# Loading x's first pair first and in halves, its norm ahead of the bias masks, and the zeros for the masked values written by ScalarE

## What is computed

```python
x = x + xattn0(layernorm(x), ctx)          # 16 heads of 16; biases bq, bk, bv, bo
x = x + ffn0(layernorm(x))                 # ternary weights, 8-bit activations
x = x + xattn1(layernorm(x), ctx)          # two attentions of 16 heads of 32, each with its own feed-forward
x = x + moe(layernorm(x))                  # 8 experts, each token goes to one
```

```python
xh = (x - mean) / sqrt(var + 1e-5)
q  = xh @ Wq + bq                          # Wq 256 x 256
k  = ctx @ Wk + bk                         # Wk 128 x 256
v  = ctx @ Wv + bv
```

## Time and profile before

| | us |
|---|---|
| median of three runs | 1157.76 |
| the three runs | 1154.86, 1157.76, 1159.51 |
| the profiled execution | 1160.95 |
| its span, first to last instruction | 1159.2 |
| TensorE busy in the span | 1056.4 |
| VectorE, ScalarE, GpSimd busy | 527.4, 459.0, 272.2 |

### The profile page before, as it was taken

How to read it: one execution, slowest core, us unless ns; L and a number is a source line. 1 busy time by engine, 2 the same in 40 slices (tenths; PEclk the granted TensorE clock), 3 DMA queues, 4 the chain that set the end, 5 groups by cost and what they waited for, 6 DMA issues and landing times. The chain is left out here.

```text
span 1159.2 us, 20650 instructions
## 1 busy us (share of the span) xinstructions
PE 1056.4 (91%) x8642; PEld 727.7 (63%) x8642; DVE 527.4 (45%) x1201; ACT 459.0 (40%) x659; POOL 272.2 (23%) x408
## 2 busy tenths in 40 slices
PE   5999974998999998999999999999999994999997
PEld 3555642554456555565766575666667663999996
DVE  5566678886347777752422333665233113000000
ACT  3757543666344444444123225554221222222221
POOL 3022301000013333323022001555311103222211
PEclk9999997999999999999999999999999995999999
DMA  8500000000051000000000020000612104856510
GB/s 248 79 2 2 2 1 0 1 1 1 1 129 18 2 2 2 2 2 1 1 1 0 1 91 1 3 2 22 197 36 81 47 19 147 327 190 196 178 55 1
DMA packets 55342, 60.55 MB, mean 52 GB/s; under 512 B 23587, under 2 KB 47055, under 8 KB 55250
## 3 DMA queue, kind: packets, MB, share of 16 engines
q1 hardware_dynamic: 52306, 52.93, 14.9%
q0 software_dynamic: 2944, 6.30, 1.8%
HBM read 54.76 MB, written 7.21 MB: 53 GB/s over the span
## 5 line engine op out<-in xcount | busy, mean ns | idle before, releaser
L648 DVE TENSOR_REDUCE small<-ps 128x16 f32<-128x1920 f32 (+1 forms) x64 | 142.2, 2221 | 62.4 <-PE ps L1271 41.0
L988 ACT ACTIVATE r_a<-ps 120x1024 f32<-120x1024 f32 (+1 forms) x128 | 124.1, 1021 | 23.8 <-PE ps L1306 23.5
L1373 PE MATMUL ps<-r_w,r_k 128*128 128x256 f32 x512 | 113.3, 381 | 1.6 <-ACT r_k L1145 1.6
L1588 PE MATMUL ps<-r_a,r_w 128*128 128x512 f32 x256 | 111.5, 593 | 3.1 <-ACT r_a L1063 3.1
L1373 PEld LDWEIGHTS ps<-r_w,r_k 128*128 128x128 f32 x512 | 96.3, 190 | 17.1 <-issue 2.9
L1324 PE MATMUL ps<-r_a,onesf 128*32 128x256 f32 (+1 forms) x768 | 90.5, 385 | 8.2 <-ACT r_a L988 8.2
L1819 PEld LDWEIGHTS ps<-feat_block,w_block 128*128 128x128 f32 x736 | 87.9, 196 | 1.5 <-ACT feat_block L1913 0.4
L1819 PE MATMUL ps<-feat_block,w_block 128*128 128x128 f32 x736 | 88.2, 280 | 0.0
L1588 PEld LDWEIGHTS ps<-r_a,r_w 128*128 128x128 f32 x256 | 48.4, 190 | 61.6 <-issue 57.4
L1905 DVE TENSOR_TENSOR rows_block<-ps,rows_block 128x256 f32<-128x256 f32 x23 | 9.8, 424 | 166.1 <-PE ps L1831 166.1
L1831 PE MATMUL ps<-w_all,hidden_block 128*128 x368 | 83.1, 379 | 0.0
(11 more groups left out here) (232 smaller groups left out, 1762.9 us busy)
## 6 DMA issues: line engine op xcount, KB each, us to landing
w_block<-in_L_ffn_W SPq DMA_DIRECT2D x23, 1024.0 KB, 6.0
w_all<-in_L_ffn_W SPq DMA_DIRECT2D x8, 1024.0 KB, 9.5
r_w<-in_L_xattn_a_li_w SPq DMA_DIRECT2D x4, 1024.0 KB, 7.3
x_all<-in_x SPq DMA_DIRECT2D x4, 512.0 KB, 7.2
x_rows<-x_all SPq DMA_DIRECT2D x4, 512.0 KB, 3.0
x_rows<-r_a SPq DMA_DIRECT2D x4, 512.0 KB, 3.0
y_all<-in_L_ffn_w_gate SPq DMA_DIRECT2D x1, 1024.0 KB, 11.1
y_all<-in_L_ffn_w_up SPq DMA_DIRECT2D x1, 1024.0 KB, 13.3
```

Source lines behind the costliest of these rows:

```text
L648: step(dve.tensor_reduce(nm.rearrange("p (j s) -> p j s", j=4), src, AX.X, ALU.max, negate=True))
L988: act.activation(PT[0:nk, 2 * x:2 * x + 2, :], bank(n % 2, 2 * x, 2)[0:nk], ACT.Exp, scale=scale).then_inc(sem["exp_done"], 1)
L1373: ins_ = pe.matmul(o[:, t // 2, (t % 2) * D:(t % 2 + 1) * D], src[:, c, t * P:(t + 1) * P], w[:, c, :], start=(c == 0), stop=(c == chunks ...
L1588: ins_ = pe.matmul(o, LI[a]["li2"][:, c, m * P:(m + 1) * P], FT3[:, c, :], start=(c == 0), stop=(c == KC - 1))
```

## The change

- x's pair 0 is loaded by the first two issues of SP's queue, two tiles each (semaphores `x0_half` and `x_loaded0`), ahead of ctx; pair 1 is issued right behind the first weights, ahead of the bias rows.
- VectorE takes the statistics of the first two tiles when the first half is there, and waits for the second before the other two.
- VectorE's norm of pair 0 and the statistics of pair 1 come before `sel`, the clearing of MX and `bk_mask`.
- GpSimd no longer clears the values' room; ScalarE does, as its first work, with one copy of ones scaled by 0 into 4096 elements.
- TensorE transposes the bias rows, and ScalarE copies them, after pair 0's transposes of ctx and x and not before.

```diff
--- before.py
+++ after.py
@@ -242,7 +242,7 @@
         def bank(h, b, n=1):
             return ps[:, 4 * h + b, :] if n == 1 else ps[:, 4 * h + b:4 * h + b + n, :]
 
-        NAMES = ["x_loaded0", "x_loaded1", "x_loaded2", "x_loaded3", "ctx_loaded", "w0_loaded", "pv_loaded", "bv0_loaded", "bv_loaded",
+        NAMES = ["x_loaded0", "x_loaded1", "x_loaded2", "x_loaded3", "x0_half", "ctx_loaded", "w0_loaded", "pv_loaded", "bv0_loaded", "bv_loaded",
                  "q_loaded0", "q_loaded1", "q_loaded2", "wo_loaded", "moe_loaded", "a1_loaded", "li_a1_loaded", "a2_loaded",
                  "ctx2_loaded", "li_a2_loaded", "x5_stored", "x5h_stored",
                  "const_ready", "masks_ready", "sel_ready", "pvT_done", "pv_ready", "bkm_ready", "vm_zeroed",
@@ -325,11 +325,14 @@
                 def x_load(p):
                     load(f"x_loaded{p}", X[p], x_rows[PS * p:PS * (p + 1), :].rearrange("(t q) n -> q t n", q=P))
 
+
+                for h, name in enumerate(("x0_half", "x_loaded0")):
+                    load(name, X[0][:, 2 * h:2 * h + 2, :], x_rows[S * h:S * (h + 1), :].rearrange("(t q) n -> q t n", q=P))
                 load("ctx_loaded", CT[0:KV], ins["ctx_512"].rearrange("b k n -> k b n"))
-                x_load(0)
                 load("w0_loaded", wk0, ins["L0_xattn_Wk"])
                 load("w0_loaded", wv0, ins["L0_xattn_Wv"])
                 load("w0_loaded", wq0, chunked("L0_xattn_Wq"))
+                x_load(1)
                 for n in PP:
                     c0, m = col[n]
                     load("pv_loaded", pv_rows[c0:c0 + m, :], ins[n].rearrange("(c p) -> c p", p=P))
@@ -337,7 +340,7 @@
                     load(name, bvec[:, k, :], ins[BC[k]].rearrange("(a n) -> a n", a=1).to_broadcast([P, D]))
 
                 rows("bv0_loaded", 0)
-                for p in range(1, NP):
+                for p in range(2, NP):
                     x_load(p)
                 load("q_loaded0", raw[0].rearrange("p (c i) -> p c i", i=D), chunked("L0_ffn_w_gate"))
                 load("q_loaded1", raw[1].rearrange("p (c i) -> p c i", i=D), chunked("L0_ffn_w_up"))
@@ -448,9 +451,7 @@
                     last = pool.affine_select(out=own_row[:, x, :], in_=own_row[:, x, :], compare_op=ALU.not_equal, fill=1.0,
                                               base=-2 * x - 1, pattern=[[-32, 4]], channel_multiplier=1)
                 last.then_inc(sem["masks_ready"], 1)
-                rstd()
-                pool.memset(view(r_q, 0, [4096]), 0.0).then_inc(sem["vm_zeroed"], 1)
-                for p in range(1, NP):
+                for p in range(NP):
                     rstd()
 
 
@@ -563,11 +564,14 @@
                     chain += 1
                     dve.wait_ge(sem["dve_chain"], chain)
 
-                def stats(src, rows=P, tiles=PT_TILES):
+                def stats(src, rows=P, tiles=PT_TILES, second=None):
+
                     nonlocal norms
                     k, at = norms, LN_W * (norms % 4)
                     norms += 1
                     for t in range(tiles):
+                        if t == 2 and second:
+                            dve.wait_ge(sem[second], 16)
                         ins_ = dve.bn_stats(sa(at + 6 * t, 6, rows), src[0:rows, t, :])
                     step(ins_)
                     for t in range(tiles):
@@ -602,20 +606,11 @@
 
 
                 dve.wait_ge(sem["const_ready"], 1)
-                dve.wait_ge(sem["x_loaded0"], 16)
-                k0 = stats(X[0])
+                dve.wait_ge(sem["x0_half"], 16)
+                k0 = stats(X[0], second="x_loaded0")
                 dve.wait_ge(sem["masks_ready"], 1)
                 dve.tensor_reduce(par_mask[:], own16[:].rearrange("p (j k) -> p k j", k=2), AX.X, ALU.add)
                 step(dve.tensor_reduce(sel_col[:], own_row[:], AX.X, ALU.add))
-                for x in range(2):
-                    ins_ = dve.tensor_scalar(sel[:, x, :], onesf[:], sel_col[:, x:x + 1], None, ALU.mult)
-                dve.memset(MX, 0.0)
-                ins_.then_inc(sem["sel_ready"], 1)
-                dve.wait_ge(sem["pv_ready"], 1)
-                for m in range(KC):
-                    ins_ = dve.tensor_tensor(bk_mask[:, 2 * m:2 * m + 2], par_mask[:], pv("L0_xattn_bk", m).to_broadcast([P, 2]),
-                                             ALU.mult)
-                ins_.then_inc(sem["bkm_ready"], 1)
                 for p in range(NP):
                     if p >= 2:
                         dve.wait_ge(sem["xT_done"], p - 1)
@@ -624,6 +619,15 @@
                         dve.wait_ge(sem[f"x_loaded{p + 1}"], 16)
                         k0 = stats(X[p + 1])
                     if p == 0:
+                        for x in range(2):
+                            ins_ = dve.tensor_scalar(sel[:, x, :], onesf[:], sel_col[:, x:x + 1], None, ALU.mult)
+                        dve.memset(MX, 0.0)
+                        ins_.then_inc(sem["sel_ready"], 1)
+                        dve.wait_ge(sem["pv_ready"], 1)
+                        for m in range(KC):
+                            ins_ = dve.tensor_tensor(bk_mask[:, 2 * m:2 * m + 2], par_mask[:],
+                                                     pv("L0_xattn_bk", m).to_broadcast([P, 2]), ALU.mult)
+                        ins_.then_inc(sem["bkm_ready"], 1)
                         dve.wait_ge(sem["vm_zeroed"], 1)
                         dve.wait_ge(sem["bv0_loaded"], 16)
                     dve.wait_ge(sem["kv0_done"], p + 1)
@@ -952,13 +956,19 @@
                     act.activation(touched[:], neghalf[:, 0:1], f)
 
 
-                act.wait_ge(sem["pvT_done"], 1)
-                act.activation(pvec[:], ps[:, 7, 0:ncol], ACT.Copy).then_inc(sem["pv_ready"], 1)
+
+                act.wait_ge(sem["const_ready"], 1)
+                act.activation(view(r_q, 0, [4096]).rearrange("p (a n) -> p a n", n=P),
+                               onesf[:].rearrange("p (o n) -> p o n", o=1).to_broadcast([P, 32, P]), ACT.Copy, scale=0.0
+                               ).then_inc(sem["vm_zeroed"], 1)
                 for p in range(NP):
                     act.wait_ge(sem["ctxT_done"], p + 1)
                     act.activation(CTT[:, PS_KV * p:PS_KV * (p + 1)], ps[:, 4, 0:PS_KV], ACT.Copy).then_inc(sem["ctxT_ready"], 1)
                     act.wait_ge(sem["xT_done"], p + 1)
                     act.activation(FTA[p % 2], ps[:, 0:2, :], ACT.Copy).then_inc(sem["ft_ready"], 1)
+                    if p == 0:
+                        act.wait_ge(sem["pvT_done"], 1)
+                        act.activation(pvec[:], ps[:, 7, 0:ncol], ACT.Copy).then_inc(sem["pv_ready"], 1)
                     act.wait_ge(sem["kv0_done"], p + 1)
                     if p == 0:
                         act.wait_ge(sem["bkm_ready"], 1)
@@ -1445,11 +1455,12 @@
                             ins_ = pe.transpose(o, w[:, c, i * P:(i + 1) * P] if k < 2 else w[:, i, c * P:(c + 1) * P], identb[:])
                     ins_.then_inc(sem["ternT_done"], 1)
 
-                pe.wait_ge(sem["pv_loaded"], 16 * len(PP))
-                pe.transpose(ps[:, 7, 0:ncol], pv_rows[0:ncol, :], ident[0:ncol, 0:ncol]).then_inc(sem["pvT_done"], 1)
                 for p in range(NP):
                     ctx_transposes(p)
                     x_transposes(p)
+                    if p == 0:
+                        pe.wait_ge(sem["pv_loaded"], 16 * len(PP))
+                        pe.transpose(ps[:, 7, 0:ncol], pv_rows[0:ncol, :], ident[0:ncol, 0:ncol]).then_inc(sem["pvT_done"], 1)
                     keys_values(p)
                     if p == NP - 1:
```

## The result

The changed kernel takes 1154.66 us (median of 22 runs, 1152.23 to 1159.14) where the kernel before, run beside it, takes 1157.11 (22 runs, 1154.86 to 1160.29). The ratio is 0.9981, with a 95% interval of 0.9972 to 0.9990: faster by 0.19%, 1 to 3 us, well under the 0.5% of the text above. (The two medians alone give 0.9979, or 2.45 us; both lie inside the interval.) The forecast was 1154.7. The profiled execution took 1157.57 us, its span is 1155.7.

A forecast was written before the change was run, and what follows sets the result against it. TensorE, busy 91% of the span, was taken to bound the kernel through the start of pair 0's keys and values. -4.2 + 0.7 + 0.4 = -3.1 us from the median 1157.76 gave 1154.7 us, range 1150.0 to 1159.0.

The forecast's parts named there:

- Norm, ScalarE's clearing, masks: Pair 0's norm on VectorE moves 5.2 us earlier; ScalarE's clearing takes 3.8 us and masks end by 15.4, both costing 0.
- Here the bias rows take over: TensorE, after x's transposes end at 11.4 us, waits for the bias rows, landing at 12.0.
- I take 12.0, by the nearest row: Bias rows' landing on SP's queue: last load issued at about 8.9 us, landing at about 12.0; keys and values -4.2 us.
- The rate: TensorE's clock rises at 16.45 us, 4.2 after unbroken work starts: keys and values +0.7 us, queries +0.4.
- (a): Transposes don't matter to TensorE's rate, which rises 1.7 us after 12.25: -4.2 us, 1153.6 us; chance 0.15.
- (b): TensorE's short hole after x's transposes is forgiven, rate up at 12.9 us: -4.7 us, 1153.1 us; chance 0.15.
- (c): Bias rows land late behind pair 1's load; loses from a 15.1 us landing, at 17.5 gives 1160.2 us; chance 0.05.
- (d): The gain is absorbed by a later load or wait tied to the start: 1157.8 us; chance 0.1.
- The Trainium skill's rule: On TensorE, transposes don't count as work for the full clock, so splitting them off costs nothing: sum -4.2 us.

The follow-up runs named there:

- e3: Changed kernel with GpSimd again clearing the values' room, behind the first factor, instead of ScalarE; median 1155.12 us, ratio to the kernel before 0.9984.
- e1: Changed kernel with TensorE transposing the bias rows behind pair 0's keys and values instead of ahead of them; median 1151.00 us, ratio to before 0.9954.
- e2: Changed kernel with x's pair 1 loaded behind the bias rows again, as in the kernel before; median 1155.50 us, ratio to before 0.9989.
- e10: Changed kernel with x's pair 0 loaded whole, still first in the queue, instead of in halves; ratio to the kernel before 0.9977.
- e4: Changed kernel's order on VectorE, ScalarE and TensorE, with the loads of the kernel before; median 1154.76 us, ratio to before 0.9977.
- e9: Changed kernel with e7's edits, and x's pair 1 load issued from ScalarE's queue instead of SP's; median 1152.25 us, ratio to before 0.9940.
- e7: Changed kernel with bias rows transposed behind keys and values, plus 24 unread TensorE transposes from 3.4 us on; median 1151.62 us, ratio to before 0.9960.
- e8: Kernel before with only its loads changed: pair 0 first in halves, ctx behind, pair 1 ahead of bias rows; median 1158.18 us, ratio 1.0009.
- e6: Changed kernel with bias rows transposed behind keys and values, plus 14 unread TensorE matmuls from 3.4 us on; median 1152.93 us, ratio to before 0.9961.

## Why the prediction was right, and where it was off

The time (1154.7 forecast, 1154.66 measured), the sign and the range held. The sum behind it held in its parts less well, and parts of the error cancel.

- **Norm, ScalarE's clearing, masks.** Right. Norm forecast for 7.8 to 9.4, measured 7.21 to 8.59. The clearing takes 3.62 us of ScalarE's idle time. The step that said VectorE's long instruction came from the clearing is shown by e3 (3515 ns).
- **"Here the bias rows take over".** Right, and the center of the case: e1 takes this wait away and gains 3 us more.
- **"I take 12.0, by the nearest row".** Off by 0.86 us: the bias rows' transpose started at 12.86. The step failed in two parts. The issues went out 1.57 us later, not 1.05, and landing took 3.4 us, not 3.1. I counted only the places in the queue; e2 and e10 point to pair 1's data ahead of the rows as well. Keys and values started at 13.12, so -3.35 us in place of -4.2.
- **The rate.** Keys and values cost +0.83 (3.47 against 2.64; forecast +0.7), the queries +0.73 (4.17 against 3.44; forecast +0.4). The rate rose 5.0 us after 13.12, the end of the range that I had from three starts in the kernel before. (The first of these, 3.5 us, is 3.7: the values' matmul of 557 ns starts at 18.07 and the fast ones at 18.46, so the rise is nearer to 18.4.) Together: -3.35 + 0.83 + 0.73 = -1.79, the shift that the timeline shows at pair 1, where I forecast -3.1.
- **The median** moved by 2.45 us, the ratio's interval is 1.2 to 3.2 us. 1.78 lies in it; so nothing more is needed, and -3.1 is at its edge. That the forecast hit the median to 0.1 us is luck: the gain was put 0.65 us too high, and the start too, since the median of three runs of before, 1157.76, became 1157.11 in 22.
- **Rivals.** (a) a rise 1.7 us after the first ordinary matmul, whatever came before: fallen, it took 5.0 in the changed kernel and 3.9 in e1. It was 1.8 us in e3 and 1.9 in e4, where the transposes stood right ahead as in the kernel before; but so they did in e1, so their place doesn't settle the moment either. (b) the hole forgiven: fallen in the changed kernel, where the transposes from 8.65 didn't bring the rate up by 18.1. In e2, with a hole of 0.74 us, it was up at about 14.6, 3.0 us after 11.61, so a short hole may be forgiven; with 3.0 us also seen in e9 from the first instruction on, this can't settle it. (c) bias rows late: they were, by 0.86 us, far from its 15.1. (d) absorbed: not so, the shift of 1.8 stays to the end of the attention. The prediction named as a sign of being wrong that the shift at the first attention unit isn't that at the end; it was 1.8 and 3.5 in the profiled pair, and what the later stretches add is in the table above.
- **The Trainium skill's rule** on transposes ("TensorE: Matmul & The Clock Gate", Part 4), that they don't count as work for the full clock: I gave it 0.15. The trace of e7 doesn't agree: after 24 transposes and two more, x's eight took 1.09 us and keys and values 1.85. After idle time x's eight took 1.97. In e9 the rate rose in the middle of 24 transposes that nothing preceded.

**What the parts of the change are worth**, from e3, e4, e8 and e10. At the start of keys and values, which the moment of the rate's rise doesn't touch, the new order on VectorE, ScalarE and TensorE gives 2.73 of the 3.35 us with the old loads (16.47 to 13.74) and the new loads 0.62 on top of it, 0.21 of them by the halves; the clearing's move gives 0.94 with the new loads. The new loads alone lose 0.20. At pair 1 the old loads (20.06), the clearing on GpSimd (20.32) and the whole load (20.51) all come ahead of the changed kernel (20.97); each is one profiled execution, and their differences are within what the moment of the rise can make. The medians of these four lie within 0.5 us. The best kernel of the case without work of no use is the changed one with e1's edit, 1151.00 us against 1157.32 of before, ratio 0.9954: it leaves nothing out. The work of no use in e6, e7 and e9 isn't shown to gain anything over it.

**Spread.** The stretch from the first gate matmul to the second layer's first scores took 172.62 us before, 171.80 after, 166.97 in e1, 174.01 in e6 and 167.14 in e9, with the same instructions in it, one profile each. In 22 runs of the changed kernel the time goes against the mean granted clock with a correlation of -0.95 (0.980 at 1152.23 us, 0.973 at 1159.14). So the run-to-run spread of 7 us goes with TensorE's rate; that the rate differs mostly in the stretches where it waits often is argued from the profiles, since the timed runs show only the mean. That e1's profiled span is 1148.3 us is in good part this.

## To carry to other kernels

When a transfer or a norm is brought forward, ask what the same engine waits for next: here six microseconds at the first step became 1.8 because a wait for small vectors, needed only later, stood behind it. Put such a wait behind the work that doesn't need it before bringing anything else forward. Where TensorE runs slow after a pause, part of the time gained ahead of the rise is lost again (here 1.56 of 3.35 us), and a kernel that starts later can end the stretch earlier, as e3, e4 and e10 did. Compare a landmark in the timeline, not only medians, when the effect is near the spread, and take one ahead of the rise as well as one behind it. Look up in the trace when a DMA was really issued: in e9 an issue written behind a long instruction went out at that instruction's start.

## What the runs showed of the hardware, not expected

- The rate rose 3.0 us (e9), 3.7 (kernel before), 3.9 (e3), 4.0 (e4), 5.0 (changed kernel) and 5.7 us (e1) after the start of unbroken work. Transposes alone brought it up (e9). In the kernel before, the changed one, e1, e3 and e4 the granted clock column showed 1.00 there all the time, while keys' matmuls took 607 ns, and 366 at the upper rate (e7); durations had to be read.
- The rate fell in e2 with an idle time of 2.03 us: x's eight transposes began at 272 ns each and ended at 421.
- Sixteen small loads of 0.5 to 4 KB release TensorE 2.35 (e2) to 4.6 us (e10) after the last one's issue.
- With 512 KB issued on ScalarE's queue at 2.48 us, ctx took 8.8 us to land on SP's in e9, where it took 5.2 in the changed kernel. It was seen once.
